# A graph network of three node stages: TensorE's products of one strip are moved against the target groups it builds for the next

## What is computed

```python
def gcn_conv(x, edge_index, W, b):
    h = x @ W
    # self loops appended to src and dst
    deg = segment_sum(ones_like(dst), dst)
    dinv = where(deg > 0, rsqrt(deg), 0)
    msg = h[src] * (dinv[src] * dinv[dst])[:, None]
    return segment_sum(msg, dst) + b
h = maximum(layernorm(x), 0)
x = x + gcn_conv(relu(gcn_conv(h, ei, W1, b1)), ei, W2, b2)
h = maximum(layernorm(x), 0)
msg = relu(concat(h[src], edge_attr) @ W1 + b1)     # 200000 x 128
agg = segment_sum(msg, dst) / maximum(count, 1)
out = x + relu(concat(h, agg) @ W2 + b2)
```

## Time and profile before

| | before |
|---|---|
| median of three runs | 2602.47 us |
| lowest, highest | 2597.78, 2609.36 us |
| span of the profiled execution | 3056.9 us |
| stage of the change (strips 1 to 24) | 434 to 1208 us |
| PE, DVE, ACT, POOL busy over the span | 80, 61, 40, 60% |

### The profile page before, as it was taken

The page is one execution under the profiler, slowest core; times in us unless marked ns, Lnnn a source line. Parts: engine busy times, 40 slices in busy tenths (PEclk is TensorE's granted clock), DMA queues, the critical chain, the costliest instruction groups (busy, mean ns, idle before and its releaser), DMA issues.

```text
span 3056.9 us, 47534 instructions
## 1 busy us (share of the span) xinstructions
PE 2439.1 (80%) x15568; PEld 1902.2 (62%) x15569; DVE 1869.8 (61%) x3558; ACT 1223.1 (40%) x3314; POOL 1820.8 (60%) x1687
## 2 busy tenths in 40 slices
PE   2774578788899888799974888888888888888787
PEld 0113356677778777588763666666666666676666
DVE  6996997566666443544453556656655565565557
ACT  6703233444566664455531333333333333333321
POOL 3745387777787664677734555555555555655560
PEclk9996699989899999799985899999998999999989
DMA  9102122232333341388842223233332323323322
GB/s 376 66 1 68 69 69 79 94 123 90 128 126 145 145 153 58 108 319 309 298 174 77 77 90 102 80 105 94 103 92 77 113 81 98 98 76 101 95 73 51
DMA packets 127022, 357.85 MB, mean 117 GB/s; under 512 B 34066, under 2 KB 77559, under 8 KB 117543
## 3 DMA queue, kind: packets, MB, share of 16 engines
q10 hardware_dynamic: 24752, 186.56, 16.0%
q0 software_dynamic: 56880, 85.25, 10.7%
q1 hardware_dynamic: 45225, 84.00, 7.9%
HBM read 229.75 MB, written 125.93 MB: 116 GB/s over the span
## 4 chain that ended last, share of the span: by engine, by line
PE 56%; DVE 16%; issue 10%; another core or an unknown queue 7%; ACT 4%; DMA 3%; DVEq 2%; POOL 1%; ACTq 0%; SPq 0%; POOLq 0%
PE ps_node L1005 6%; PE ps_feat L1005 5%; PE ps_node L1020 5%; PE ps_sum L1107 4%; PE ps_extra L1145 4%; PE ps_feat L1020 4%; PE pre_banks L993 4%; PE pre_banks L1098 3%; PE ps_node L1133 2%; PE ps_node L1129 2%; PE ps_extra L993 2%; DVE region_c L1877 2%; PE ps_sum L1129 2%; PE ps_sum L1133 2%
## 5 line engine op out<-in xcount | busy, mean ns | idle before, releaser
L741 POOL DMA_INDIRECT rows<-table,region_a x800 | 784.4, 981 | 639.5 <-issue 222.6
L759 POOL DMA_INDIRECT permuted<-rows_or_lows,slot_of_edge x768 | 883.5, 1150 | 410.0 <-issue 157.5
L1145 PE MATMUL ps_extra<-msg_parts,target_hot 128*128 128x256 f32 x1176 | 234.4, 317 | 163.6 <-DVE msg_parts L2040 105.4
L1877 DVE TENSOR_TENSOR region_c<-iota_key,region_c 128x1568 bf16<-128x1568 f16 (+1 forms) x327 | 355.8, 1088 | 0.0
L1318 ACT ACTIVATE region_a<-pre_banks 128x392 bf16<-128x392 f32 x392 | 194.5, 499 | 248.2 <-PE pre_banks L993 147.9
L1145 PEld LDWEIGHTS ps_extra<-msg_parts,target_hot 128*128 128x128 f32 x1176 | 169.5, 199 | 181.7 <-DVE msg_parts L2040 117.5
L1005 PE MATMUL ps_node<-region_a,region_b 128*128 128x256 bf16 (+1 forms) x1911 | 277.5, 276 | 3.8 <-issue 2.4
L1005 PE MATMUL ps_feat<-region_a,region_b 128*128 128x256 bf16 x1764 | 259.4, 276 | 2.1 <-issue 1.4
L2055 DVE TENSOR_TENSOR target_hot<-consts,region_a 128x512 fp32r<-128x512 f32 x336 | 207.3, 617 | 58.6 <-PE ps_extra L1145 39.5
L1107 PE MATMUL ps_sum<-onehot,rows 128*128 128x64 f32 x1600 | 221.3, 286 | 13.5 <-issue 13.3
L1107 PEld LDWEIGHTS ps_sum<-onehot,rows 128*128 128x128 f32 x1600 | 217.5, 210 | 19.8 <-issue 18.4
(11 more groups left out here) (273 smaller groups left out, 5202.6 us busy)
## 6 DMA issues: line engine op xcount, KB each, us to landing
counts<-region_a ACTq DMA_DIRECT2D x23, 3136.0 KB
region_a<-counts ACTq DMA_DIRECT2D x11, 3200.0 KB
region_a<-counts ACTq DMA_DIRECT2D x11, 3072.0 KB
rows_or_lows<-block_lows ACTq DMA_DIRECT2D x72, 448.0 KB
permuted<-region_b SPq DMA_DIRECT2D x25, 833.0 KB
region_a<-permuted SPq DMA_DIRECT2D x24, 833.0 KB
rows_or_lows<-edge_cols_in POOLq DMA_DIRECT2D x24, 544.0 KB
region_a<-attr_t_in SPq DMA_DIRECT2D x50, 256.0 KB
```

The lines of the kernel that those rows point to most:

```text
L741: nc.gpsimd.indirect_dma_start(rows[:, s, j * D:(j + 1) * D], None, tables[2], bass.IndirectOffsetOnAxis(ap=message_rows[:, c * TC + j:c * ...
L759: nc.gpsimd.indirect_dma_start(permuted, bass.IndirectOffsetOnAxis(ap=slot_of_edge[:, r * RT + k:r * RT + k + 1], axis=0), edge_rows_of[:, ...
L1145: last = mm(ps_extra[:, 0:2 * D], target_hot[:, u % 2, j], msg_parts[:, u % 2, j].rearrange("p h d -> p (h d)"), start=(u % DU == 0 and j ...
L1877: v.tensor_tensor(hot_key(u)[:, :, 0:n], iota_key[:, None, 0:n].to_broadcast([P, UNIT // SIDE, n, SIDE]), keys[:, :, None, :].to_broadcast ...
```

## The change

In each strip from 1 on, the first windows 0 to 2 are built with no products behind them; behind window 3 stand the two waits, and the 49 blocks of products are spread over windows 3 to 27; windows 28 to 31 are built with none. (In strip 24, of 14 windows, the products stand behind windows 3 to 9.) The products of a strip thus end four windows before it does.

```diff
--- before.py
+++ after.py
@@ -1030,16 +1030,16 @@
                     for strip in range(STRIPS):
                         other = 1 - strip % 2
                         windows = windows_of(strip)
-                        if strip:
-                            pe.wait_ge(C["evacuated"], strip * SW + BANKS)
-                            pe.wait_ge(strip_added[other], (strip + 1) // 2)
+                        alone = (BANKS - 1, len(windows) - 1 - BANKS)
                         for j, w in enumerate(windows):
                             build_window(w)
-                            if strip:
-                                for h in range(j * (SB - 1) // len(windows), (j + 1) * (SB - 1) // len(windows)):
+                            if strip and j == alone[0]:
+                                pe.wait_ge(C["evacuated"], strip * SW + BANKS)
+                                pe.wait_ge(strip_added[other], (strip + 1) // 2)
+                            if strip and alone[0] <= j <= alone[1]:
+                                of, span = j - alone[0], alone[1] - alone[0] + 1
+                                for h in range(of * SB // span, (of + 1) * SB // span):
                                     apply(other, h)
-                        if strip:
-                            apply(other, SB - 1)
                     pe.wait_ge(C["evacuated"], NW + BANKS)
                     pe.wait_ge(strip_added[(STRIPS - 1) % 2], (STRIPS + 1) // 2)
                     for h in range(SB):
```

## The result

| | median, us | lowest to highest | ratio to before, 95% interval |
|---|---|---|---|
| before | 2600.78 | 2597.78 to 2609.36 | |
| changed | 2614.41 | 2611.79 to 2620.73 | 1.0058 [1.0030, 1.0085] |
| changed, a second time, twelve executions | 2613.96 | 2605.81 to 2621.08 | 1.0047 [1.0026, 1.0068] |

What follows compares the result with a forecast made beforehand. PE bounds the stage; its idle time at strip boundaries is what can be won. Terms 4.2 + 6.1 − 1.8 − 3.3 + 1.7 = +6.9 us gave 2609.4 us on the median, range 2584 to 2622 us.

Steps and rivals of the forecast that it cites:

- Reading of the disturbed trace: First profile of the kernel before: signals up to 8 us late and long gaps were a recording cost, absent from timed runs.
- The faster rival: Four-matmul boundaries: late signals are the kernel's own, so the change wins 9 to 25 us, middle 2585 us; chance 0.22.
- Regular strips: Six boundaries after strips 9 to 14: DVE's add starts 0.9 us after the last product (T); +0.70 each, +4.2 us.
- Four-matmul strips: Six boundaries after strips 3 to 8: idle falls from 1.41 to 1.11 us, −0.30 each, −1.8 us.
- the recurrence: Four-matmul boundary worked build by build: one-hot units ready 2.28 and 3.81 us after the strip's last product, 1.11 us idle.
- Late strips: Nine boundaries after strips 15 to 23: bare builds wait for ACT's evictions, 1.20 us idle against 0.52; +0.68 each, +6.1 us.
- 0.11 more: Late boundaries, window 4: PE waits 0.11 us for window 0's eviction, which stands behind the store's DMA issue on ACT.
- The end of strip 24: Four bare builds end the strip and the closing products wait for the fourth bank: +1.7 us.
- Strips 1 and 2: DVE sets the pace; with products ending four windows earlier its waits of 1.83 and 1.48 us go: −3.3 us.
- What a measurement can tell: Whole kernel: below 0.5% (13 us) a measurement cannot tell a change from none.
- The rival of the clock: Late strips: PE's clock falls in the bare stretch, +10.9 us over nine boundaries, 2620 us; slower rival, chance 0.18.

Runs made afterwards that it cites:

- the second profile: The kernel before, profiled again with no edit; ratio 0.9999 [0.9979, 1.0019] of before.
- the late add: The change, with DVE's add of a strip moved behind the first eight windows' one-hots of the strip after next; 2608.98 us, 1.0022 of before.
- ahead_only: Against the change: four bare windows ahead of the products, none behind (products behind windows 3 to 31); 2638.04 us, 1.0133 of before.
- late_store: The change with the store's issue on ACT moved behind the first four evictions of the next strip; 2610.16 us, a single execution.

## Why the prediction was right in kind and half in size

- **Reading of the disturbed trace: right.** Taking the gaps of the earlier trace rows for no part of the timed runs, and the costs from strips with no lateness, gave 1.41, 0.84 and 0.52 us where the second profile has 1.43, 0.84 and 0.53. The faster rival rested on the other reading and fell with it. The rule of the Trainium skill (NOTIFIC — the notification-queue block, section 10, Constraints, capacities, measured rates) that emitting an implicit record costs the engine no cycles is neither borne out nor refuted: the eleven later profiles lie within 1% of the timed runs, one lay 17% above. What I drew from it, that the late signals would then be the kernel's own, was wrong: the same kernel showed none the second time.
- **Regular strips: right.** +0.70 us predicted, 28.28 to 28.98 measured in five of the six boundaries (for the sixth see strip 10 below); DVE's add 0.8 us after T (forecast 0.9) with no wait before it.
- **Four-matmul strips: right.** −0.30 predicted, −0.36 measured per strip; the gaps at T+2.3 and T+3.8 stand where the recurrence had them. The step from strip 2 to 3 alone went the other way (29.32 to 29.68). A slip stands in the working: by its own prices PE reaches the middle of window 3 at 3.00, not 2.82; nothing hangs on it, since the unit comes at 3.81.
- **Late strips: the step that failed.** The term said "0.11 more" for window 4. I gave window 3 two blocks of products (0.66 us, "about two blocks each"); the code's rounding gives it one, so PE arrives 0.33 us sooner. And ACT takes up 0.23 us after the issue's end (1013.56 to 1013.79), 1.19 us after window 31 and not 0.95. The first products came when I had them, T+2.62 (forecast 2.61); window 4 followed at T+3.57, 0.62 us after the block. That is +1.22 to +1.29 for +0.68 at the seven boundaries with a second wait, +0.75 after strip 15, and +1.5 after strip 23. There the kernel before had no gap at all (strip 24's 14 windows have three and four blocks each behind them), where I had counted one of 0.52. Over the nine it is 11.0 us for 6.1, without the dip of the clock below.
- **A term left out: the passage into strip 10.** I counted it as one more regular boundary, +0.70. In the change the first wide unit, which DVE can only start late, stands ahead of the add, and PE waits a second time, 1.58 us:

```profile
690.46 0.41 DVE L1902 TENSOR_TENSOR agg<-agg,ps_node 128x256 f32<-128x256 f32 x1
...
693.65 0.85 PE L993 MATMUL ps_extra<-region_c 128*128 128x392 bf16 x2 [1.58 <-DVE region_c L1877]
```

The two strips 9 and 10 took 2.38 us more, where −0.30 and +0.70 were forecast. Their idle time rose by 0.9 us (4.10 to 5.03); the rest goes with the clock, granted at 0.90 in strip 10 against 0.95 before.

- **The end of strip 24: right.** 1.66 predicted; the closing products waited 1.65 us:

```profile
1080.77 7.40 PE L1005 MATMUL ps_node<-region_a,region_b 128*128 128x112 bf16 x147 [1.65 <-ACT region_a L1318]
```

- **Strips 1 and 2: right by the sum.** DVE's waits before its adds are gone, and strip 2 took 36.33 us, not 38.19. Of the 4.69 us of the table four builds of 0.36 us are only moved behind T, so some 3.2 are won for the 3.3 forecast. The granted clock was 0.96 there before and 1.00 in the change; what part of the gain is the clock's no run separates.
- **The 8.7 us between 6.9 and 15.6.** The late boundaries give 4.9 of them, strip 10 gives 2.0, the dip of the clock below 1.8; the other terms cancel to 0.2.
- **What a measurement can tell: wrong.** I wrote that below 0.5% this kernel's change can't be told from none. 0.47% was told, with an interval of 1.0026 to 1.0068.
- **The rival of the clock: small.** The granted clock of the late strips is 1.00 but for one:

```profile
913.87:939.50 25.63, 24.43 (x213) 21.29 (x212) 12.82 (x17) 18.06 (x65) 19.93 (x19) 0.93 0.37 139
```

One dip, 1.8 us, where the rival wanted every second boundary. It is no accident: the second profile of the change and that with the late add have it at the same strip. There ACT starts window 0's eviction 1.47 us after window 31's instead of 1.19, PE waits 0.74 us instead of 0.46, and the granted clock falls right behind; why ACT is later at that one boundary no run shows. In ahead_only the clock fell behind four of the five gaps of 2.15 us in the regular strips and behind one of the nine of 1.84 in the late ones. The warning of the Trainium skill (TensorE: Matmul & The Clock Gate, section "A second HAM failure mode: psum-queue depth-cycling") gives no size; the trace agrees with it at one of the late boundaries and not at the others.

## What to carry to other kernels

Work put next to a wait to cover it must not itself depend on another engine: in the late strips eight builds at 0.19 us behind an eviction every 0.48 traded DVE's chain for ACT's. Look first at what stands ahead of the late work in the slow engine's own queue: moving one add behind eight windows of one-hots was worth 1%, with TensorE's order untouched. Where products are dealt out by integer shares, write down the shares at both ends of the stretch before costing it. And where a bracket names one engine, look at what the other engines finished just before: twice here it named ACT where DVE's unit had ended 0.15 us earlier and the bank had long been free.

## What was not expected of the hardware

ACT started nothing for 0.23 us after the end of its own DMA issue (1013.56 to 1013.79), on top of the issue's 0.33; with the issue placed where its wait had been met (late_store) neither showed. An eviction of 128x392 with its row sum follows another at 0.47 to 0.49 us, though the activation and the accumulator's read are 0.50 and 0.20 us long: the read lies beside the next activation. And a profile of a program on one core was once 17% longer than its timed runs, with TensorE's signals late by up to 8 us; no other profile here showed it.
